# One fused layer on one core: lane chain ahead of the last four tiles, half of the gated sums on TensorE, 21 load buffers, 60 scatters over a stage border

## The chip, the cores and the metric

The kernel runs on one NeuronCore of a Trainium2 chip. The metric is the device time of one execution in microseconds (us); the median of three runs of the kernel before is 5569.49 us (5564.7 to 5574.14). The engines are called PE (TensorE matmul; PEld its weight loads), DVE (VectorE), ACT (ScalarE), POOL (GpSimd) and SP (SyncE, which here only issues transfers). A q behind an engine's name (SPq, ACTq) is its queue of transfers.

## The reference, cut to what matters

There are 12,500 nodes of 256 features and 212,500 edges sorted by destination. What concerns the change is the last part: every node is sent through four experts, and a graph attention over the edges (4 heads, 4 values a head) gives the scores by which the best two experts are weighted.

```python
xn = _layernorm(x); x = x + gnn(xn, edges) + mix(xn[None])[0]
x_flat = _layernorm(x)
h = (x_flat @ W_gat).reshape(M, HEADS, NUM_EXPERTS)
a_src, a_dst = (h * att_src).sum(-1), (h * att_dst).sum(-1)
e = leaky_relu(a_src[src] + a_dst[dst], 0.2)
ee = exp(e - segment_max(e, dst)[dst])
agg = segment_sum(h[src] * ee, dst) / segment_sum(ee, dst) + b_gat
w = softmax(top_k(_layernorm(agg).mean(heads), 2))
out = sum(g[e] * (gelu(x_flat @ W1[e] + b1[e]) @ W2[e] + b2[e]) for e in experts)
x = x + out
```

## The kernel before, in words

The nodes are 100 tiles of 125 rows (`NT`, `NP`). The program is a row of blocks with a barrier of all engines between them: a short setup, a graph stage (about 200 to 2801 us) in which POOL fetches the rows of the edges' sources (L773) while PE, DVE and ACT sum them, do the mixing layer and sort the edges, and a last block (from 2811 us).

In the graph stage each finished tile leaves 28 numbers a node for the router (`router_row`, L918 to L921). At its end POOL issues one scatter a tile (`ad_rows`, L778), which writes the destination's part of the score to every edge's place; the scatters t = 0 to 99 stand behind the last row fetch, each waits for its own tile.

In the last block four chains run side by side, each engine in the order of its own code:
- PE does 25 groups of four tiles: the first expert layer in 16 chunks (L1660, two matmuls each), then the second layer, 16 matmuls a tile (L1668). ACT's gelu (L1629) turns a chunk into `hid`; DVE adds the bias (L1603) and SP stores the tile's four expert outputs, 512 KB, to `y_rows` (L1295).
- POOL fetches the routers' rows of all sources (`nb`, L1339): 1024 gathers in 16 batches of 64, over `NBUF` = 3 buffers. `AHEAD` = 4 semaphores bound how many are in flight. A buffer comes free when DVE's `records` of its batch has read it (L1414).
- DVE does `scores(b)` at the tile `unit_after(b)` and `records(b)` one tile later: a running maximum, ACT's Exp, 20 scans over the lane (L1418). The records go to HBM. The tiles are 8, 16, 20, 25, 32, 36, 44, 48, 53, 60, 65, 72, 76, 84, 88 and 93.
- After batch 15 the lane chain joins the 128 lanes (functions `lane_ends`, `over_lanes`, `lane_sums`, `first_maxima`, `first_records`), one piece a tile at tiles 94 to 98, with four PE transposes (L1674) ahead of the last group's first layer, two (L1679, L1680) after its first tile, and two small Exp on ACT. It ends in a fetch and a scatter of one record a lane on POOL (L1345, L1348).

Then comes the tail. POOL fetches each tile's last records (`res`, L1355), SP loads the nodes' own rows (`own`, L1309). `weigh(k)` on DVE makes the gates of 20 tiles (`FT`), with three ACT functions between. `combine(t)` on DVE is four scalar-times-tensor-plus-tensor instructions (L1589) over the tile's four expert outputs (L1312) and residual (L1313), which SP loads into `YR` = 8 buffers once all y stores have landed. ACT's queue stores the result (L1649, two transfers a tile) from `AR` = 4 buffers.

## Time and profile before

| what | value |
|---|---|
| median of three runs | 5569.49 us |
| profiled execution, time and span | 5532.89 us, 5531.1 us |
| granted clock over the span | 0.804 |
| PE busy | 3498.8 us, 63% |
| POOL busy | 2828.8 us, 51% |
| DVE busy | 2089.8 us, 38% |
| ACT busy | 793.1 us, 14% |
| HBM read and written | 392.03 MB, 146.74 MB |

The busy shares are means over stages with different limits, so the rows below are taken by stage: the border of the two blocks, the groups of the last block with and without POOL's gathers, the last four tiles, and the tail in which PE no longer works. The times stand from the span's start.

### The profile page before, as it was taken

Reading aid. Unit: us, or ns where it says so; the run is one execution under the profiler, and the core shown is the slowest. Engines: PE = TensorE matmul, PEld = TensorE weight load, DVE = VectorE, ACT = ScalarE, POOL = GpSimd, SP = SyncE. Lnnn points to the kernel's source line nnn. Section 1 sums busy time; section 2 is a strip of 40 time slices with the busy share of each in tenths; the row PEclk is TensorE's granted clock in tenths of the full one; section 3 lists DMA queues with packets and bytes.
Section 4 is the critical chain, followed back from the end, with each engine's and each line's share of the span. In section 5 each row is a group of like instructions: output and inputs, shape, how many; then the busy total and the mean of one; then the engine's idle time right before and its main releaser. Section 6 shows DMA issues by size and latency. Waiting matters only on the chain.

```text
span 5531.1 us, 46201 instructions
## 1 busy us (share of the span) xinstructions
PE 3498.8 (63%) x12938; PEld 2286.8 (41%) x12938; DVE 2089.8 (38%) x4906; ACT 793.1 (14%) x1914; POOL 2828.8 (51%) x2951
## 2 busy tenths in 40 slices
PE   0688888888577777777242766666666666669300
PEld 0455555555455545555121443434343434346200
DVE  5466665566466545444110111202021111103288
ACT  4111111111011111111010101111111111112000
POOL 2666666666666666666657044445445353530420
PEclk6799999899788889888575888787778878789755
DMA  7444444444355555555121011111111111111287
GB/s 241 127 116 114 114 114 114 111 115 113 109 137 147 149 143 157 167 150 147 23 57 19 32 49 33 47 35 44 38 43 46 36 46 36 46 31 63 85 258 258
DMA packets 381412, 540.56 MB, mean 98 GB/s; under 512 B 120314, under 2 KB 297818, under 8 KB 381143
## 3 DMA queue, kind: packets, MB, share of 16 engines
q0 software_dynamic: 119136, 234.44, 17.7%
q1 hardware_dynamic: 239503, 284.45, 15.8%
q10 hardware_dynamic: 22632, 20.15, 1.1%
q8 instruction: 45, 0.74, 0.1%
q14 instruction: 96, 0.79, 0.0%
HBM read 392.03 MB, written 146.74 MB: 97 GB/s over the span
## 4 chain that ended last, share of the span: by engine, by line
PE 24%; another core or an unknown queue 13%; issue 7%; DVE 3%; DVEq 2%; DMA 1%; ACT 0%; SPq 0%; ACTq 0%
PE PS L1668 14%; PE PS L1660 10%; DVE acc L1589 2%; DVEq L1588 1%; DMA out<-acc 1%; ACT hid L1629 0%; DMA x2g<-x_turned 0%; DVE rec L1418 0%; DVE y_sb L1603 0%; DVE sc L1553 0%; SPq L1287 0%; DVE rden L1528 0%; ACTq L1649 0%; DVE q L1523 0%
## 5 line engine op out<-in xcount | busy, mean ns | idle before, releaser
L773 POOL DMA_INDIRECT rows<-xn_rows,gsrc x1664 | 1606.2, 965 | 881.2 <-issue 455.9
L1339 POOL DMA_INDIRECT nb<-route_rows,idx x1024 | 999.6, 976 | 1082.8 <-DVE msg L1414 767.7
L1668 PE MATMUL PS<-arena,hid 128*125 128x256 f32 x3200 | 771.0, 400 | 555.6 <-ACT hid L1629 339.4
L1078 PE MATMUL PS<-rows,oh 128*128 128x257 f32 x3328 | 891.2, 421 | 281.5 <-issue 207.2
L1660 PE MATMUL PS<-x2g,arena 128*128 128x500 f32 x1600 | 754.6, 631 | 284.8 <-issue 148.3
L1668 PEld LDWEIGHTS PS<-arena,hid 128*125 128x125 f32 x3200 | 632.8, 199 | 710.7 <-issue 578.9
L1603 DVE TENSOR_TENSOR y_sb<-PS,b_b 125x512 f32<-125x512 f32 x200 | 128.7, 685 | 2004.6 <-PE PS L1668 1467.7
L1078 PEld LDWEIGHTS PS<-rows,oh 128*128 128x128 f32 x3328 | 684.9, 212 | 411.3 <-issue 242.9
L1660 PEld LDWEIGHTS PS<-x2g,arena 128*128 128x128 f32 x1600 | 319.6, 203 | 698.7 <-issue 535.7
L1629 ACT ACTIVATE hid<-PS,b_sb 128x500 f32<-128x500 f32 x400 | 270.3, 677 | 1547.5 <-PE PS L1660 758.5
L1150 PE MATMUL PS<-own_w,p_t 128*125 128x512 f32 x400 | 237.2, 678 | 124.4 <-issue 68.8
L814 DVE TENSOR_TENSOR oh<-PS,rel 128x1024 f32<-128x1024 f32 x208 | 254.0, 1221 | 9.8 <-issue 1.8
L1095 PE MATMUL PS<-arena,x_t 128*125 128x512 f32 x400 | 223.3, 686 | 1.9 <-issue 1.9
L827 DVE TENSOR_REDUCE ss<-sq 125x16 f32<-125x1024 f32 x100 | 121.7, 1217 | 271.9 <-ACT sq L1028 193.6
L1097 PE MATMUL PS<-arena,x_t 128*125 128x512 f32 x400 | 191.0, 600 | 0.6 <-issue 0.6
L844 DVE TENSOR_TENSOR oh_lo<-PS,arena 128x500 bf16<-128x500 f32 x256 | 171.3, 669 | 0.0
L844 DVE TENSOR_TENSOR oh_hi<-PS,arena 128x400 bf16<-128x400 f32 x256 | 144.5, 564 | 61.0 <-remote 44.9
L1589 DVE SCALAR_TENSOR_TENSOR acc<-arena,gate,acc 125x256 f32<-125x256 f32 x300 | 145.4, 485 | 35.6 <-issue 14.0
L1022 ACT ACTIVATE kept<-PS 128x257 f32<-128x257 f32 x104 | 40.2, 386 | 827.8 <-remote 708.4
L1355 POOL DMA_INDIRECT res<-rec_rows,end_i x100 | 96.7, 967 | 116.0 <-DVE q L1523 84.9
L1113 PE MATMUL PS<-oh_lo,oh_hi 128*100 128x125 bf16 x1024 | 103.0, 235 | 76.1 <-issue 45.7
L1027 ACT ACTIVATE sq<-PS 125x512 f32<-125x512 f32 x100 | 59.7, 597 | 607.6 <-PE PS L1097 345.3
(303 smaller groups left out, 3093.0 us busy)
## 6 DMA issues: line engine op xcount, KB each, us to landing
y_rows<-y_sb SPq DMA_DIRECT2D x100, 512.0 KB
arena<-y_rows SPq DMA_DIRECT2D x100, 512.0 KB
rows<-xn_rows,gsrc POOLq DMA_INDIRECT x1664
nb<-route_rows,idx POOLq DMA_INDIRECT x1024
sum_rows<-kept SPq DMA_DIRECT2D x104, 128.5 KB
x_rows<-x SPq DMA_DIRECT2D x100, 128.0 KB
hid<-x_rows SPq DMA_DIRECT2D x100, 128.0 KB
m_in<-sum_rows SPq DMA_DIRECT2D x100, 125.5 KB
```

The lines of the kernel that those rows point to most:

```text
L773: pool.indirect_dma_start(out=rows[w][h][:, q, 0:D], out_offset=None, in_=xn_rows, in_offset=bass.IndirectOffsetOnAxis(ap=gsrc[:, s * HU + ...
L814: v.tensor_tensor(oh[w][h][:], NUMBERS.rearrange("p (o n) -> p o n", o=1).broadcast_to([P, HU, P]), along(rel[h][:], P), ALU.is_equal).the ...
L844: last = v.tensor_tensor(to[:, 4 * h:4 * h + 4, :], NUMBERS[:, 0:n].rearrange("p (o n) -> p o n", o=1).broadcast_to([P, 4, n]), along(of[: ...
L1078: last = mm(SUM[:, 0:D + 1], oh[w][h][:, q, :], rows[w][h][:, q, :], start=h == 0 and q == 0, stop=h == 1 and q == HU - 1)
L1095: mm(KP[0:NP, :], x_t[u][:, k * NP:(k + 1) * NP], wkv[:, k, 0:INNER], start=k == 0, stop=k == 1)
L1097: last = mm(VP[u][0:NP, :], x_t[u][:, k * NP:(k + 1) * NP], wkv[:, k, INNER:2 * INNER], start=k == 0, stop=k == 1)
L1150: both = lambda k: mm(GM[u][0:NP, :], p_t[q][:, k * NP:(k + 1) * NP], own_w[:, k, :], start=k == 0, stop=k == 1)
L1339: pool.indirect_dma_start(out=nb[b % NBUF][:, c, :], out_offset=None, in_=route_rows, in_offset=bass.IndirectOffsetOnAxis(ap=idx[:, b * W ...
L1589: last = v.scalar_tensor_tensor(out=acc[t % AR][:], in0=y_in[q][0:NP, e * D:(e + 1) * D], scalar=gate[:, t, e:e + 1], in1=acc[t % AR][:] i ...
L1629: a(hid[:, c, :], HP[c % 4][:, 0:4 * NP], ACT.Gelu, bias=b1_sb[:, c:c + 1]).then_inc(s_hid, 1)
L1660: last = mm(HP[c % 4][:, 0:4 * NP], w1_sb[:, k, e, (c % 4) * P:(c % 4 + 1) * P], x2g[u][:, k, :, :].rearrange("p j n -> p (j n)"), start=k ...
L1668: last = mm(Y[j % 2][e // 2][0:NP, (e % 2) * D:(e % 2 + 1) * D], hid[:, 4 * e + k, j * NP:(j + 1) * NP], w2_sb[:, e, k, :], start=k == 0, ...
```

## The change

It has six parts.
- **Scatters.** `ADS_EARLY` = 40: the scatters of tiles 0 to 39 stay in the graph stage, those of 40 to 99 stand at the start of the last block on POOL, ahead of the first `nb` gather. SP's load of what they wrote moves from the head of its queue to the sixth tile's store, and DVE's `start_ad` from tile 5 to tile 9 (by `unit_after(0)` - 3).
- **Batches.** `unit_after` now gives the tiles 12, 17, 24, 29, 36, 41, 48, 53, 60, 68, 72, 80, 84, 92 and 93, and sets the last batch behind all tiles; it is done with the lane chain. `AHEAD` is 8. `records` drains DVE between its 20 scans.
- **Lane chain.** `LANES_AT` = 96: behind tile 95's copy DVE does the last batch's scores and records and the whole chain in one piece; ACT does the batch's Exp ahead of the last group's gelus; PE's transposes (`turn_ends`) stand between the last group's two layers. `weigh(0)` stands ahead of the copies of tiles 98 and 99.
- **Gated sum.** In the tail, for every even tile ACT writes four diagonal matrices (the identity times a gate), PE multiplies them with the tile's four outputs into a PSUM bank, and DVE adds the residual in one instruction. Odd tiles are as before. `FT` is 10, and `weigh(k + 1)` stands ahead of the tiles of group k.
- **Buffers.** `YR` is 21 (five of their own, the others in space that is free by then), `AR` is 10, waited for by threes and pairs; the first five y tiles and `own(0)` are loaded at tile 95.
- **Queues.** `own(k + 2)` is loaded by ACT's queue and no longer by SP's. The stores of a tile stand ten tiles later on it.

Besides, `sort_low` and `sort_high` of the graph stage stand at other places of DVE's half step.

```diff
-YR = 8
-AR = 4
-FT = 20
+SPARE = 5
+YR = SPARE + 16
+AR = 10
+FT = 10
-AHEAD = 4
+AHEAD = 8
+ADS_EARLY = 40
+LANES_AT = NT - 4
 def unit_after(b):
-    t = int((b + 1) * 5.65) + 3
-    return t if t % 4 < 2 else t + 4 - t % 4
+    t = int((b + 1) * 6.06 + 5.5)
+    t = t if t % 4 < 2 else t + 4 - t % 4
+    return NT if b == NB - 1 else min(t, LANES_AT - 3)
...
-                for t in range(NT):
+                for t in range(ADS_EARLY):
                     pool.wait_ge(s_hc, t + 2)
...
+                    if t == 6:
+                        sp.wait_ge(s_ads, 16 * NT)
+                        sp.dma_start(ad[:], ad_rows[0:EF, :].rearrange("(p f) h -> p f h", p=P)).then_inc(s_adl, 16)
...
+                    if t == LANES_AT - 1:
+                        for b in late:
+                            store_records(sp, b)
+                        load_own(sp, 0)
+                        for i in range(AT_PE):
+                            load_y(i)
...
+                for t in range(ADS_EARLY, NT):
+                    pool.indirect_dma_start(out=ad_rows, out_offset=bass.IndirectOffsetOnAxis(ap=start_i[:, t:t + 1], axis=0),
+                                            in_=ad_all[:, t, :], in_offset=None).then_inc(s_ads, 16)
...
                     for k in range(20):
+                        if k:
+                            v.drain()
...
+                def add_rows(t):
                     q = t % YR
+                    dve.wait_ge(loaded(t), in_group(t))
                     if t >= AR:
+                        dve.wait_ge(stored(t), (t // AR) * 64)
+                    if t % 2 == 0:
+                        dve.wait_ge(s_cmb, t // 2 + 1)
+                        v.tensor_tensor(acc[t % AR], CMB[t // 2 % CB][0:NP, 0:D], x1_in[q][0:NP, :], ALU.add).then_inc(s_acc, 1)
+                        return
...
+                    if t == LANES_AT - 1:
+                        for b in late:
+                            scores(b)
+                            records(b)
+                        lane_ends()
+                        over_lanes()
+                        lane_sums()
+                        first_maxima()
+                        first_records()
+                    if t == NT - 3:
+                        weigh(0)
                 for k in range(FG):
-                    weigh(k)
+                    if k + 1 < FG:
+                        weigh(k + 1)
                     for t in range(k * FT, (k + 1) * FT):
-                        combine(t)
+                        add_rows(t)
...
+                        if t == k * FT:
+                            act.wait_ge(s_gt, k + 1)
+                            if k + 2 < FG:
+                                load_own(act, k + 2)
+                        if t % 2 == 0:
+                            if t // 2 >= DG:
+                                act.wait_ge(s_cmb, t // 2 - DG + 1)
+                            for e in range(NE):
+                                last = a(diag[t // 2 % DG][:, e, :], ident[0:NP, 0:NP], ACT.Copy, scale=gate[:, t, e:e + 1])
+                            last.then_inc(s_diag, 1)
+                        if t >= FT:
+                            store_out(t - FT)
...
+                def turn_ends():
+                    pe.wait_ge(s_ends, 1)
+                    for k in range(4):
+                        last = nc.tensor.transpose(HP[0][0:20, k * P:(k + 1) * P], ends[:, k, :], ident)
+                    last.then_inc(s_endt, 1)
+                    pe.wait_ge(s_ends, 2)
+                    nc.tensor.transpose(HP[1][:, 0:20], fm[:, 0:P], ident[0:20, 0:20])
+                    nc.tensor.transpose(HP[1][:, 20:40], fx[:, 0:P], ident[0:20, 0:20]).then_inc(s_endt, 1)
...
+                    if isinstance(g, int) and 4 * g == LANES_AT:
+                        turn_ends()
...
+                for t in range(0, NT, 2):
+                    pe.wait_ge(loaded(t), in_group(t))
+                    pe.wait_ge(s_diag, t // 2 + 1)
+                    if t // 2 >= CB:
+                        pe.wait_ge(s_acc, t - 2 * CB + 1)
+                    for e in range(NE):
+                        last = mm(CMB[t // 2 % CB][0:NP, 0:D], diag[t // 2 % DG][:, e, :], y_in[t % YR][0:NP, e * D:(e + 1) * D], start=e == 0, stop=e == NE - 1)
+                    last.then_inc(s_cmb, 1)
```

How the instructions stand on an engine is shown by its list in program order: line, operation, out<-in with the shape, semaphores waited for, and a count. First POOL at the border of the two blocks, before (L778 the scatters, L1339 the gathers of the first batch):

```order
L778 DMA ad_rows<-ad_all,start_i 143872x4 [waits s_hc] x100
L609 UNCONDITIONAL_BRANCH
L1325 UNCONDITIONAL_BRANCH [waits barrier_Pool_Activation_PE_DVE_SP_gather]
L1327 MEMSET first_e 125x16
L1329 AFFINE_SELECT first_e<-first_e 125x16 [waits s_fe]
L1331 DMA ad_first<-route_rows,first_i 128x28
L1339 DMA nb<-route_rows,idx 128x28 x4
```

And POOL at the same border after the change (L787 and L1369 the scatters, L1379 the gathers):

```order
L787 DMA ad_rows<-ad_all,start_i 143872x4 [waits s_hc] x40
L618 UNCONDITIONAL_BRANCH
L1362 UNCONDITIONAL_BRANCH [waits barrier_Pool_Activation_PE_DVE_SP_gather]
L1364 MEMSET first_e 125x16
L1366 AFFINE_SELECT first_e<-first_e 125x16 [waits s_fe]
L1369 DMA ad_rows<-ad_all,start_i 143872x4 x60
L1371 DMA ad_first<-route_rows,first_i 128x28
L1379 DMA nb<-route_rows,idx 128x28 x8
```

Sixty scatters moved behind the barrier and ahead of the first gather.

PE in the last group before: the lane chain's transposes (L1674) stand ahead of the first layer (L1660; its first chunk waits for DVE's copy of them, s_endc), and L1679 and L1680 behind the first tile of the second layer (L1668).

```order
L1668 MATMUL PS<-arena,hid 125x256 x15
L1674 MATMUL PS<-wide,ends 20x128 [waits s_ends]
L1674 MATMUL PS<-wide,ends 20x128 x3
L1660 MATMUL PS<-x2g,arena 128x500 [waits s_hid,s_x2l0,s_endc]
...
L1668 MATMUL PS<-arena,hid 125x256 x15
L1679 MATMUL PS<-wide,fm 128x20 [waits s_fx]
L1680 MATMUL PS<-wide,fx 128x20
L1668 MATMUL PS<-arena,hid 125x256 [waits s_yc]
```

PE in the last group after, from the end of the first layer (L1745) over the second (L1755) to the first gated sums (L1773):

```order
L1745 MATMUL PS<-x2g,arena 128x500
L1733 MATMUL PS<-wide,ends 20x128 [waits s_ends,s_hid]
L1733 MATMUL PS<-wide,ends 20x128 x3
L1736 MATMUL PS<-wide,fm 128x20 [waits s_ends]
L1737 MATMUL PS<-wide,fx 128x20
L1755 MATMUL PS<-arena,hid 125x256 [waits s_yc]
...
L1773 MATMUL PS<-spare_y,nb 125x256 [waits s_diag,s_yl0,s_yc]
L1773 MATMUL PS<-spare_y,nb 125x256 x3
```

All six transposes now stand between the two layers, and the second layer's 64 matmuls are behind both waits for DVE (s_ends).

DVE after, from the copy of tile 97 (L1649) to the first tiles of the tail: weigh(0) begins at L1548 and ends with the gates at L1620, L1630 is an even tile, L1635 an odd one.

```order
L1649 TENSOR_TENSOR y_sb<-PS,b_b 125x512
L1548 TENSOR_TENSOR zf<-res,own 125x40 [waits s_res0,s_own]
...
L1620 TENSOR_TENSOR gate<-sx,m 125x40
L1649 TENSOR_TENSOR y_sb<-PS,b_b 125x512 [waits s_ys0,s_y]
...
L1620 TENSOR_TENSOR gate<-sx,m 125x40
L1630 TENSOR_TENSOR nb<-PS,hid 125x256 [waits s_cmb,s_yl0]
L1635 SCALAR_TENSOR_TENSOR nb<-spare_y,gate,hid 125x256 [waits s_yl0]
L1635 SCALAR_TENSOR_TENSOR nb<-spare_y,gate,nb 125x256 x3
```

Before, all of `weigh` stood behind the copy of tile 99; now the copies of tiles 98 and 99 are behind the wait for the first `own` and `res`.

## Rows read from the trace of the kernel before

**Rows 1.** Costliest groups of the page: operation, count | busy, mean ns | idle, releaser
```profile
L1339 POOL DMA_INDIRECT nb<-route_rows,idx x1024 | 999.6, 976 | 1082.8 <-DVE msg L1414 767.7
```

**Rows 2.** Windows: start:end, us, busy PE, PEld, DVE, ACT, POOL, PEclk, DMA, GB/s
```profile
2822.00:2852.00 30.00, 29.07 (x63) 13.05 (x64) 0.00 (x0) 9.41 (x13) 20.74 (x22) 0.89 0.29 89
2852.00:3064.00 212.00, 46.55 (x99) 25.43 (x97) 2.58 (x4) 2.71 (x4) 156.58 (x165) 0.53 0.11 19
3091.00:3192.00 101.00, 99.38 (x339) 63.48 (x338) 24.54 (x37) 23.58 (x34) 0.00 (x0) 1.00 0.13 45
...
5250.00:5531.00 281.00, 0.00 (x0) 0.00 (x0) 234.00 (x537) 13.93 (x20) 39.23 (x40) 0.50 0.81 258
5173.00:5531.00 358.00, 0.00 (x0) 0.00 (x0) 255.03 (x590) 17.41 (x25) 91.64 (x95) 0.50 0.72 226
```

**Rows 3.** Timeline inside the first burst: start, us, engine, line, [idle before <-releaser]
```profile
2899.20 0.59 PE L1668 MATMUL PS<-arena,hid 128*125 128x256 f32 x1 [2.42 <-issue]
...
2902.00 0.59 PE L1668 MATMUL PS<-arena,hid 128*125 128x256 f32 x1 [2.21 <-issue]
```

**Rows 4.** What POOL's gathers (L1339) waited for: us, times
```profile
  DMA nb<-route_rows,idx: 13.8, 23
```

**Rows 5.** The scatters of the border (L778): ns min/median/max, first and last start
```profile
L778 POOL DMA_INDIRECT ad_rows<-ad_all,start_i x100: 965/969/1053, 2620.8 to 2800.9; - x100
...
  issue: 27.4, 90
```

**Rows 6.** Timeline of the last eight tiles, columns as in rows 3
```profile
5074.95 27.89 PE L1668 MATMUL PS<-arena,hid 128*125 128x256 f32 x128 [0.77 <-ACT hid L1629]
...
5090.27 0.16 DVE L1385 COPY m_run<-m_run 128x4 f32<-128x4 f32 x1
...
5096.14 0.63 ACT L1633 ACTIVATE dd<-dd 128x512 f32<-128x512 f32 x1 [19.94 <-DVE dd L1401]
...
5099.64 5.32 DVE L1418 TENSOR_TENSOR_SCAN rec<-dd,rec,msg 128x64 f32<-128x64 f32 x20
...
5105.52 1.03 PE L1674 MATMUL PS<-wide,ends 128*20 128x128 f32 x4 [2.67 <-DVE ends L1432]
...
5108.35 29.04 PE L1660 MATMUL PS<-x2g,arena 128*128 128x500 f32 x64 [1.81 <-DVE endt L1448]
...
5111.40 0.42 ACT L1636 ACTIVATE dc<-dc 20x256 f32<-20x256 f32 x1 [14.63 <-DVE dc L1463]
```

**Rows 7.** Timeline from the last tile into the tail
```profile
5166.44 0.97 POOL L1355 DMA_INDIRECT res<-rec_rows,end_i  x1 [1.51 <-DMA rec_rows<-fix,put_i]
...
5168.84 1.29 DVE L1603 TENSOR_TENSOR y_sb<-PS,b_b 125x512 f32<-125x512 f32 x2 [5.19 <-issue]
...
5173.20 4.57 SPq L1312 DMA_DIRECT2D arena<-y_rows  x1
```

**Rows 8.** Timeline of the tail's steady part, columns as in rows 3
```profile
5252.31 0.48 DVE L1589 SCALAR_TENSOR_TENSOR acc<-arena,gate,hid 125x256 f32<-125x256 f32 x1
...
5254.39 0.48 DVE L1589 SCALAR_TENSOR_TENSOR acc<-arena,gate,hid 125x256 f32<-125x256 f32 x1
...
5269.01 7.67 SPq L1312 DMA_DIRECT2D arena<-y_rows  x1
...
5283.41 0.23 DVE L1506 TENSOR_TENSOR zf<-res,own 125x80 f32<-125x80 f32 x1
```

**Rows 9.** Timeline, first tile after the second weigh
```profile
5300.45 0.48 DVE L1589 SCALAR_TENSOR_TENSOR acc<-arena,gate,hid 125x256 f32<-125x256 f32 x1 [0.15 <-issue]
```

**Rows 10.** Groups by line: operation, count | busy, mean ns | idle before
```profile
L900 DVE TENSOR_TENSOR x<-x,PS 125x256 f32<-125x256 f32 x100 | 42.2, 422 | 7.5
...
L1016 ACT ACTIVATE x_t<-PS 128x250 f32<-128x250 f32 x100 | 39.8, 398 | 53.4 <-PE PS L1087 37.0 <-remote 16.5
...
L1044 ACT ACTIVATE ssq<-ssq 125x1 f32<-125x1 f32 x100 | 20.3, 203 | 6.8
```

**Rows 11.** Out stores on ACT's queue (L1649): ns min/median/max
```profile
L1649 ACTq DMA_DIRECT2D out<-acc x200: 322/371/1539, 5233.6 to 5529.1; - x100
```

More of the change, by code:

```diff
@@ L1325, in _ @@
+                for q in range(AR // 2):
+                    sp.wait_ge(s_out[q], 64 * NT // AR)
             @block.gpsimd
@@ L1497, in first_records @@
                     v.drain()
[L1498 removed]
+                    v.tensor_tensor(fix[:, 0:20], fix[:, 0:20], back[:, 1, :], ALU.add).then_inc(s_fix, 1)
                 def weigh(k):
```

154 lines of the change are left out of this document (80 added, 74 removed).

## The prediction

> **What bounds the kernel now.** I read the page's groups first, then windows cut at the borders of the stages, then the timelines of the last tiles and of the tail; a mean over the whole span would mix four different limits. In the last block PE is the bound where POOL is quiet: it is busy 99.38 of 101 us in the window from 3091 [rows 2]. Where POOL runs a long row of gathers, PE is not the bound and not waited for either: after the first 30 us of such a row (29.07 busy) it does 46.55 us of work in 212 [rows 2], and the reader is to see its matmuls 2.80 us apart with "issue" as the only reason [rows 3]. So a long row of POOL transfers costs PE about 0.78 of what lies behind its first 30 us. From 5173 on PE has nothing, the granted clock is 0.50 (the 1.2 GHz level), and two limits run close together: DVE is busy 234.0 of 281 us, the transfers 0.81 at 258 GB/s [rows 2]. A tile takes DVE 2.07 us (5252.31 to 5254.39), one `weigh` of 20 tiles 17.04 us (5283.41 to 5300.45) [rows 8, 9].
>
> **The zero of the sum.** Tile 95's matmuls end at 5074.95 + 27.89 = 5102.84 [rows 6]. Seen from there the span before ends at 5531.1 - 5102.84 = +428.3, and the y loads begin at 5173.20, +70.4 [rows 7].
>
> **The border of the stages.** Ninety scatters stand back to back, each 0.969 us and an issue gap of 27.4 / 90 = 0.30, so 1.27 us apart [rows 5]; the last ten come with their tiles. With 40 scatters, 50 of the ninety leave, 64 us. The engines' part behind them (2734 to 2801) shifts forward by about that, since PE, DVE and ACT stood nearly still meanwhile. In the last block 60 x 1.27 = 76 us stand ahead of the gathers. POOL's first row so ends 12 us later; but PE now starts on the first group 64 us earlier and works at 46.55 / 212 = 0.22 during the 76 us more, 17 us of work. The sum is 12 - 17 = -5, and I take 0 with 10 to each side. `ad` and `start_ad` come later, by tile 6 and tile 9; they have until tile 12.
>
> **Batches, eight in flight, drains.** POOL waited for its own gathers 23 times, 13.8 us of 1082.8 idle [rows 1, 4]; nearly all the rest is DVE's `records`. Eight in flight can win at most these 13.8. The thirteen later rows of 64 stay thirteen, at other tiles: 0, with 10 to each side for the cover that each finds. The drains make the 20 scans longer: 5.32 us is 0.27 a scan now, overlapped [rows 6]; apart, a step of DVE of this size takes near 0.46 (an addition of 0.42 and its gap), so 19 x 0.19 = 3.6 us a batch, hidden on DVE, which does little between two copies of PE's tiles; only the last batch shows it. Moving the sorts in DVE's half step of the graph stage changes the order, not the work: 0, with 10 to each side.
>
> **The lane chain.** Before: last tile's copy at 5168.84, first `res` at 5166.44 [rows 7]. After, from tile 95: `records(14)` ends about +6, the copy +7.3, `scores(15)` takes 5.9 (5090.27 to 5096.14 [rows 6]) to +13.2, Exp 0.63 and a table load until +15.4. Until then no gelu of the last group runs, and PE has only four PSUM banks for its first layer; it stalls 8.6 us behind chunk 4. (The layer before took 29.04 with about 2 us of such a stall.) The first layer so ends about +36.2, `hid` +36.9. `records(15)`, 8.7 with drains 12.3, is done by then. The transposes, the pieces between and the small Exp took from 5105.52 to 5111.82 [rows 6], 6.3 us, and the sums another 0.6: PE waits 6.9 us, to +43.8, and ends its four tiles 27.9 later at +71.7, against +66.0. What waits behind: only these four tiles. The record's fetch and scatter go ahead beside them; the first `res` starts about +50, ten have landed at +65. `weigh(0)` takes to +81, then come the copies of tiles 98 and 99 (+84) and the loads at +86.3: 16 us later than before. Price of a `weigh` of ten tiles: between half of 17.04 and all of it; its instructions are many and short, so I take 12.8.
>
> **The tail.** `own(1)` lands about +93, and `weigh(1)`, with ACT's first matrices ahead of its Exp, ends at +114. From there on DVE has 50 odd tiles at 2.07, and 50 even ones: one addition of 125x256 from PSUM, 0.42 [rows 10], 0.50 with its gap. That is 50 x 2.57 = 128.5; eight more `weigh` 102.4; 2.4 for the last store: +347. Ten us for waits (nothing to 26, which is 0.1 of the window) give +357.
> ACT's side: a diagonal matrix is 125x125, between the 0.203 us of a one-column and the 0.398 of a 250-column instruction [rows 10], I take 0.30; four of them and four stores at 0.371 [rows 11] are 2.7 us a pair, with both bounds 2.3 to 3.1. This is as long as DVE's pair of 2.57; but ACT goes on during `weigh`, so it sets nothing unless it is at the upper end, 50 x 0.5 = 26 us. PE's side: 27.89 / 16 = 1.74 us for four matmuls at full clock, 3.5 at the clock 0.50 of the tail: 17.5 a group against DVE's 25.6.
> Transfers: 0.72 x 358 = 258 us of full work before [rows 2], less about 8 for the five y tiles loaded ahead, 250. Between +86 and +347 they would have to be busy 0.96; with +357, 0.92. With 8 buffers they reached 0.81, in a window where SP's queue stood 7.67 us on the y load behind `own` [rows 8]; 21 buffers and `own` on another queue are there to bridge this. I take 0.92.
>
> On that queue a rule of the Trainium skill bears (DMA: Bandwidth & Descriptors, "Issuing engines are not separate DMA queues"): whichever engine starts a transfer, it runs on the same 16 engines, and another issuer saves only issue time. By it the move of `own` is worth nothing; were the hold of 7.67 us wholly gone each time, it would be ten such holds, and the sum above counts none of them.
>
> **The sum.** -71 us in the last part (+428.3 to +357), 0 elsewhere. The profiled execution took 5532.9, so 5462; the median of the runs shown stands 36.6 above it, and I forecast 5569.5 - 71 = 5498.
>
> **Rivals.**
> A. The transfers stay where they were, 0.81: 250 / 0.81 = 309 from +86, +395. It gains 33: 5536. For it: the share did not follow DVE's load, and more loads and stores in flight share the same engines. Against: before, a load could go out only when one of 8 buffers came free, and there were stretches in which none was.
> B. Slower: eight gathers in flight take PE's cover. If the first 30 us of each row shrink because POOL's gathers are issued closer, or because more of them are under way, PE loses 0.78 x 15 = 12 us a row at half the cover, 13 rows 152 us: -71 + 152 = +81, 5650. It decides above 5.5 us a row. Against: POOL issues one each 1.25 us and waited for a landing only 23 times [rows 4].
> C. ACT, PE and DVE run one after another: ACT's Exp of the next `weigh` stands behind the group's matrices and stores, which wait for PE's sums and DVE's tiles. With 8 us lost in each of nine groups, 72 us, nothing is gained: 5570. For it: ACT's pair is as long as DVE's. Against: PE's 17.5 us a group have 25.6.
> D. POOL's rows do not slow PE by what they issue. The scatters moved over the border would cost the last block nothing while the graph stage is 64 us shorter: 5498 - 64 = 5434. Against: PE's 46.55 us in 212 stand right beside them [rows 2].
> The Trainium skill (Runtime: NRT & Kernel Launch, "Instruction fetch mechanics") says that instructions are fetched ahead by a queue of each engine's own and that this is hidden; by it D would hold. The trace does not agree: 2.80 us between matmuls of 0.59 [rows 3].
>
> **Chances.** Forecast 0.52, A 0.22, D 0.08, C 0.08, B 0.08, and 0.02 for a border that costs more than the tail gives. A measurement of this kernel tells 0.2% (11 us) from nothing: faster 0.82, the same 0.08, slower 0.10. The forecast's own range is 5470 to 5525, by the waits (0 to 26), ACT's upper end and the border; with A and D and their own spread 5430 to 5560, which leaves out C's upper half and B.
>
> **What would show it.** Right: PE's last second layer begins 44 us behind tile 95 and the loads 86; the last block opens about 64 us earlier and its first group ends where it did, within 10; DVE's tail has pairs of about 2.6 us with no wait of more than 1 us ahead of an even tile, and a transfer share above 0.9. Wrong in the tail: "DMA" or PE's sum (L1773) as the releaser of most tiles. Wrong in the groups: rows of 64 in which PE slows before its twentieth us. The prediction fails as a whole if the border is not neutral, since there 60 to 76 us stand against each other.

## The result and the profile after

The changed kernel takes 5612.55 us (median of 4 runs, 5608.44 to 5618.63) against 5569.4 (5564.7 to 5574.14) before: 1.0078 times, interval 1.0065 to 1.009. It is 43 us slower; 71 us faster was forecast, and the time lies above the range.

The table holds this and every later run. The stages are cut at the same instructions in each kernel: *rows* from the first to the last row fetch of the graph stage, *border* from there to the first group's last copy, *groups* to tile 91's copy, *last 8* to tile 99's copy, *tail* to the end (us). The last column is of the 13 later rows of 64 gathers: from a row's start to the end of the last gelu that comes in time, which is the last one before a gap of over 2 us (median), and how many gelus (chunks of the first layer) ACT does in all 13. All are worked out from the traces. The ratio is to the kernel before, run in the same set (several kernels and that one, on one chip). That kernel took 5569.4, 5526.19, 5560.91, 5533.57, 5560.59 and 5535.58 us in the six sets, so kernels of different sets are compared by ratio.

| kernel | ratio (interval) | rows | border | groups | last 8 | tail | late gelu / gelus |
|---|---|---|---|---|---|---|---|
| before | 1 | 2485 | 473 | 1955 | 121 | 362 | 22.4 / 176 |
| after | 1.0078 (1.0065-1.009) | 2513 | 480 | 2031 | 153 | 304 | 17.3 / 113 |
| after_again | 1.0085 (1.0068-1.0102) | 2508 | 476 | 2029 | 153 | 304 | 17.3 / 116 |
| e1_no_drains | 0.9976 (0.996-0.9991) | 2478 | 474 | 1959 | 145 | 304 | 20.7 / 174 |
| e2_ahead4 | 1.0040 (1.0024-1.0055) | 2498 | 480 | 1983 | 153 | 310 | 15.7 / 136 |
| e3_old_sorts | 1.0041 (1.0023-1.0058) | 2469 | 476 | 1998 | 153 | 316 | 15.7 / 129 |
| e4_before_drains | 1.0074 (1.0054-1.0094) | 2481 | 468 | 1982 | 126 | 363 | 15.5 / 128 |
| e5_own_sp | 1.0031 (1.0016-1.0046) | 2514 | 478 | 2028 | 153 | 276 | 17.2 / 116 |
| e6_ads100 | 1.0098 (1.0077-1.0119) | 2508 | 475 | 2024 | 153 | 300 | 15.8 / 116 |
| e7_all_dve | 1.0169 (1.0148-1.0189) | 2501 | 478 | 2033 | 153 | 357 | 17.2 / 113 |
| c1_four_undone | 0.9882 (0.9865-0.99) | 2470 | 479 | 1948 | 145 | 277 | 22.4 / 179 |
| c2_ahead8 | 0.9900 (0.9884-0.9917) | 2474 | 482 | 1959 | 145 | 272 | 20.7 / 175 |
| c3_weigh_behind | 0.9883 (0.9864-0.9902) | 2473 | 485 | 1954 | 144 | 277 | 22.5 / 181 |
| c4_new_sorts | 0.9906 (0.9891-0.9921) | 2486 | 479 | 1950 | 145 | 277 | 22.4 / 180 |
| d1_drains_ahead | 0.9900 (0.9883-0.9917) | 2514 | 480 | 1965 | 148 | 272 | 23.9 / 180 |
| d2_longer_dve | 0.9727 (0.971-0.9743) | 2507 | 480 | 1859 | 154 | 271 | 27.4 / 203 |
| d3_with_drains | 1.0017 (1.0007-1.0027) | 2509 | 479 | 2022 | 153 | 274 | 16.5 / 119 |
| d4_with_drains_ahead8 | 1.0020 (1.001-1.0031) | 2504 | 479 | 2029 | 152 | 271 | 16.5 / 117 |
| f1_pause16 | 0.9428 (0.9401-0.9454) | 2484 | 476 | 1696 | 153 | 275 | 22.4 / 209 |
| f2_pause8 | 0.8622 (0.8607-0.8638) | 2484 | 329 | 1237 | 304 | 278 | no late gelu |

The forecast's 71 us were a gain of 89 in the tail (273 us, from the copies at +84 to the end at +357, against 362) less 18 in the last eight tiles (+84 against +66). The tail won 58, the last eight tiles lost 32, and the groups lost 76 where nothing was expected. These are differences of two profiled executions: the one of before took 5532.9 us, 36.6 under its median, the one after 5618.6, and the stages together differ by 86 us where the medians differ by 43. So the groups' 76 can be more than the change costs there, and prices are taken from the ratios. (The rows stage stands 44 us apart in c1 and d1, which do the same in it on two chips, and 20 in e1 and e2 on one; single differences there are not read.)

The gathers of the last block (columns as in [rows 1]) and windows (as in [rows 2]) of the changed kernel: POOL's first row, a stretch in which POOL is quiet, the tail.

```profile
L1379 POOL DMA_INDIRECT nb<-route_rows,idx x1024 | 985.2, 962 | 1280.5 <-DVE msg L1454 972.2
```
```profile
2799.00:3096.00 297.00, 68.78 (x127) 33.03 (x125) 2.58 (x4) 6.10 (x9) 227.22 (x230) 0.54 0.12 15
3128.00:3285.00 157.00, 154.53 (x532) 99.84 (x532) 30.31 (x47) 34.47 (x50) 0.00 (x0) 1.00 0.17 60
5313.00:5617.00 304.00, 125.73 (x400) 91.91 (x400) 196.78 (x594) 93.74 (x245) 74.76 (x77) 0.69 0.82 259
```

In the first row PE does 68.78 us of work in 297, 0.23 of it, as the 0.22 of [rows 2]; with POOL quiet it is busy 154.53 of 157. Those two readings held. DVE is busy 196.78 of the tail's 304, less than the 234.0 of 281 of [rows 2]; the transfers reach 0.82, not 0.92.

What the groups lost shows in one later row of 64, which begins at 3592.75 before and at 3581.41 after. ACT's gelus in it (start, us, engine, line, [idle before <-releaser]), before and after:

```profile
3610.94 0.68 ACT L1629 ACTIVATE hid<-PS,b_sb 128x500 f32<-128x500 f32 x1 [1.00 <-PE PS L1660]
3612.62 0.68 ACT L1629 ACTIVATE hid<-PS,b_sb 128x500 f32<-128x500 f32 x1 [1.00 <-issue]
3615.84 0.68 ACT L1629 ACTIVATE hid<-PS,b_sb 128x500 f32<-128x500 f32 x1 [2.55 <-remote]
3627.08 0.68 ACT L1629 ACTIVATE hid<-PS,b_sb 128x500 f32<-128x500 f32 x1 [7.03 <-remote]
3638.27 0.68 ACT L1629 ACTIVATE hid<-PS,b_sb 128x500 f32<-128x500 f32 x1 [10.51 <-remote]
...
3660.67 0.68 ACT L1629 ACTIVATE hid<-PS,b_sb 128x500 f32<-128x500 f32 x1 [10.52 <-remote]
```
```profile
3594.48 1.28 ACT L1694 ACT_TABLE_LOAD   x1 [16.45 <-remote]
3598.02 0.68 ACT L1694 ACTIVATE hid<-PS,b_sb 128x500 f32<-128x500 f32 x1 [2.26 <-remote]
3602.97 0.68 ACT L1694 ACTIVATE hid<-PS,b_sb 128x500 f32<-128x500 f32 x1 [4.27 <-remote]
3610.00 0.68 ACT L1694 ACTIVATE hid<-PS,b_sb 128x500 f32<-128x500 f32 x1 [6.35 <-remote]
3620.53 0.68 ACT L1694 ACTIVATE hid<-PS,b_sb 128x500 f32<-128x500 f32 x1 [9.85 <-remote]
```

Before, they come 1.68 us apart until 3612.62, 20 us into the row, and only then farther and farther apart. After, the first one is 16.6 us into the row and already late. (The two rows begin at different points of a group: PE's first layer starts 2.9 us into the row before and, by its own rows, 9.8 after. Most rows of before start as the latter, and in those the first late gelu comes 23 us or more into the row.) "remote" names no releaser in this program. PE's rows in the same row before:

```profile
3595.65 26.99 PE L1660 MATMUL PS<-x2g,arena 128*128 128x500 f32 x64
3661.48 9.57 PE L1668 MATMUL PS<-arena,hid 128*125 128x256 f32 x35 [38.84 <-ACT hid L1629]
```

All 64 records of the first layer's 16 chunks lie before 3622.64: PE runs up to four chunks ahead of ACT, one for each PSUM bank. The last four gelus read sums that are ready and still come 11.2 us apart, and PE's 38.84 us are a wait for the last of them, at 3660.67. So the late engine here is ACT, and the gelus are counted.

DVE at the end of that batch's `records`, after and in the kernel without drains:

```profile
3581.23 8.97 DVE L1460 TENSOR_TENSOR_SCAN rec<-dd,rec,msg 128x64 f32<-128x64 f32 x20
3590.10 1.28 DVE L1649 TENSOR_TENSOR y_sb<-PS,b_b 125x512 f32<-125x512 f32 x2
```
```profile
3522.55 5.32 DVE L1458 TENSOR_TENSOR_SCAN rec<-dd,rec,msg 128x64 f32<-128x64 f32 x20
3527.76 1.28 DVE L1647 TENSOR_TENSOR y_sb<-PS,b_b 125x512 f32<-125x512 f32 x2
```

The scans take 8.97 us for 5.32 (as in [rows 6]): +3.65, the 3.6 of the prediction. POOL at the start of the row, before (with DVE's scans there) and after:

```profile
3592.58 5.32 DVE L1418 TENSOR_TENSOR_SCAN rec<-dd,rec,msg 128x64 f32<-128x64 f32 x20
3592.75 0.99 POOL L1339 DMA_INDIRECT nb<-route_rows,idx  x1 [37.20 <-DVE msg L1414]
3594.05 1.00 POOL L1339 DMA_INDIRECT nb<-route_rows,idx  x1 [0.30 <-issue]
3595.36 3.33 POOL L1339 DMA_INDIRECT nb<-route_rows,idx  x1 [0.30 <-issue]
3598.99 0.94 POOL L1339 DMA_INDIRECT nb<-route_rows,idx  x1 [0.30 <-issue]
```
```profile
3581.41 1.00 POOL L1379 DMA_INDIRECT nb<-route_rows,idx  x1 [86.66 <-DVE msg L1454]
3582.71 1.05 POOL L1379 DMA_INDIRECT nb<-route_rows,idx  x1 [0.30 <-issue]
3584.07 1.05 POOL L1379 DMA_INDIRECT nb<-route_rows,idx  x1 [0.30 <-issue]
3585.42 1.05 POOL L1379 DMA_INDIRECT nb<-route_rows,idx  x1 [0.30 <-issue]
```

Before, the third gather is held for 3.33 us and ends at 3598.69, 0.8 us after the 20 back-to-back scans; with a drain between the scans none is held. It is a pause in POOL's issuing, six microseconds into the row, that the drains took away.

### The profile page after: what moved, and what is told of

The parts are those of the page before. It is cut to its first block, busy times and chain, and to the rows that moved or that the text cites. A ratio compares the mean times of both kernels' runs of the same rounds, so it can differ in the third digit from the quotient of the medians.

```text
span 5616.7 us, 47651 instructions
## 1 busy us (share of the span) xinstructions
PE 3708.8 (66%) x13337; PEld 2411.3 (43%) x13338; DVE 2074.5 (37%) x4946; ACT 860.6 (15%) x2135; POOL 2819.1 (50%) x2951
## 4 chain that ended last, share of the span: by engine, by line
PE 20%; another core or an unknown queue 13%; issue 11%; DVE 3%; ACT 1%; DVEq 1%; DMA 1%; SPq 1%; ACTq 0%
PE PS L1755 11%; PE PS L1745 9%; DVE nb L1635 1%; ACT hid L1694 1%; DVEq L1634 0%; ACTq L1682 0%; SPq L1322 0%; ACT nb L1719 0%; DVE rec L1460 0%; DMA ad<-y_rows 0%; ACT L1694 0%; DMA arena<-y_rows 0%; DVE z L1404 0%; DVE m_run L1428 0%
## 5 line engine op out<-in xcount | busy, mean ns | idle before, releaser
L1379 POOL DMA_INDIRECT nb<-route_rows,idx x1024 | 985.2, 962 | 1280.5 <-DVE msg L1454 972.2
L1745 PE MATMUL PS<-x2g,arena 128*128 128x500 f32 x1600 | 844.2, 685 | 604.1 <-ACT hid L1694 306.2
L1086 PE MATMUL PS<-rows,oh 128*128 128x257 f32 x3328 | 921.2, 433 | 285.9 <-ACT kept L1030 147.0
L1755 PE MATMUL PS<-arena,hid 128*125 128x256 f32 x3200 | 747.2, 392 | 348.3 <-issue 181.2
L1649 DVE TENSOR_TENSOR y_sb<-PS,b_b 125x512 f32<-125x512 f32 x200 | 128.7, 686 | 2099.1 <-PE PS L1755 1681.6
L1086 PEld LDWEIGHTS PS<-rows,oh 128*128 128x128 f32 x3328 | 708.0, 219 | 425.3 <-issue 213.4
L1755 PEld LDWEIGHTS PS<-arena,hid 128*125 128x125 f32 x3200 | 619.1, 194 | 488.7 <-issue 349.6
L1745 PEld LDWEIGHTS PS<-x2g,arena 128*128 128x128 f32 x1600 | 337.2, 218 | 1093.8 <-issue 693.5
L1113 PE MATMUL PS<-k_sb,v_sb 125*128 125x128 f32 x800 | 119.9, 298 | 73.0 <-DVE v_sb L845 54.2
```

What stands on the lines that cost most here:

```text
L1086: last = mm(SUM[:, 0:D + 1], oh[w][h][:, q, :], rows[w][h][:, q, :], start=h == 0 and q == 0, stop=h == 1 and q == HU - 1)
L1379: pool.indirect_dma_start(out=nb[b % NBUF][:, c, :], out_offset=None, in_=route_rows, in_offset=bass.IndirectOffsetOnAxis(ap=idx[:, b * W ...
L1649: last = v.tensor_tensor(y_sb[t % 2][0:NP, half * 512:half * 512 + 512], Y[t % 2][half][0:NP, :], b2_b[:, half * 512:half * 512 + 512], AL ...
L1745: last = mm(HP[c % 4][:, 0:4 * NP], w1_sb[:, k, e, (c % 4) * P:(c % 4 + 1) * P], x2g[u][:, k, :, :].rearrange("p j n -> p (j n)"), start=k ...
L1755: last = mm(Y[j % 2][e // 2][0:NP, (e % 2) * D:(e % 2 + 1) * D], hid[:, 4 * e + k, j * NP:(j + 1) * NP], w2_sb[:, e, k, :], start=k == 0, ...
```

## Experiments

The first four share a set. The changed kernel was not run in it, so a difference to the changed kernel is one of two ratios on two chips (1.0078 in the first set, 1.0085 in the one of after_again). The theories are named in words where they are judged. Where an expectation speaks of PE's cover, that is the time from a row's start to PE's first gap over 2 us in the trace: 30.3 us before, 20.6 after, 30.8 in c1, 34.3 in d2, 64.3 in f1 (means of 13 rows). The gelus of the table are the more direct measure, since PE runs ahead of ACT and then waits for it.

**e1_no_drains**, of the changed kernel:
```diff
-                        if k:
-                            v.drain()
```


> The changed kernel without the drains between the 20 scans of records; all else as changed. Theory 1 (the drains keep DVE 12.2 us a batch in place of 8.5, and PE, which has two pairs of PSUM banks for its tiles, waits for the copies): the scans take about 5.3 us again, the tiles behind a batch no longer take 12 to 13 us, PE's stall behind chunk 4 of the last group shrinks from 19 to about 9 us, and the time falls by some 60 to 85 us, to about 5530 to 5550. Theory 2 (eight gathers in flight shorten PE's cover in a row of 64): the rows cost what they do now, about 61 us each, and the time falls by less than 25 us.

Measured 0.9976, 0.0102 or 56 us below the changed kernel. The groups take 1959 us again, with 174 gelus in the rows for 113: the drains are the largest loss. In the set itself e3, with drains and with the old order of the sorts, stands 0.0065 or 36 us above e1. DVE's lateness alone could be that price, 13 x 3.65 = 47 us; d1 and d2 part the two. In the last group drains cost by lateness alone. PE at tile 95 and behind it, after and without drains:

```profile
5215.41 6.87 PE L1745 MATMUL PS<-x2g,arena 128*128 128x500 f32 x16
5241.62 21.86 PE L1745 MATMUL PS<-x2g,arena 128*128 128x500 f32 x48 [19.34 <-ACT hid L1694]
```
```profile
5101.38 6.87 PE L1743 MATMUL PS<-x2g,arena 128*128 128x500 f32 x16
5120.14 21.91 PE L1743 MATMUL PS<-x2g,arena 128*128 128x500 f32 x48 [11.89 <-ACT hid L1692]
```

The stall behind chunk 4 is 19.34 us with drains and 11.89 without: two batches of scans stand there, 2 x 3.65 = 7.3.

**e2_ahead4**, of the changed kernel:
```diff
-AHEAD = 8
+AHEAD = 4
```


> The changed kernel with four gathers in flight in place of eight. Theory 1 (drains): within 10 us of the changed kernel, 5612. Theory 2 (eight in flight): about 5 us less for each of 13 rows, 5545 to 5560.

Measured 1.0040: 21 us better by the ratios. But e3, which keeps eight in flight and has the old sorts, comes out the same on this chip, and its groups take 1998 us against 1983 here; so the 21 us may be the chip's. In c2 eight in flight cost 7 us and in d4 nothing.

**e3_old_sorts**, of the changed kernel, the two sorts back at the end of DVE's half step:
```diff
-                    (0, 0, SORTED_AT, sort_low),
...
-                    (2, 0, NT, spread), (0, 0, SORTED_AT, sort_high),
+                    (2, 0, NT, spread),
...
+                    (0, 0, SORTED_AT, sort_low), (0, 0, SORTED_AT, sort_high), (0, 0, SORTED_AT, sort_turn)], plain=SORTED_AT)
```


> The changed kernel with the two sort steps at their old places in DVE's half step of the graph stage. The profile of the changed kernel reaches the last row gather of the graph stage 29 us later than that of before. Theory 3 (the new order of the sorts delays each half step): 20 to 29 us faster, and the last row gather starts near 2620. Rival (the profile of before was a short one, 37 us under its median, and the order is neutral): within 10 us of 5612, last row gather between 2620 and 2650.

Measured 1.0041, 20 us better than the changed kernel; but the groups, in which nothing is sorted, are 33 us shorter, so this run alone does not show it: an unlike edit, e2, gives the same on the same chip. c4 asks again.

**e4_before_drains**, of the kernel before:
```diff
                     for k in range(20):
+                        if k:
+                            v.drain()
```


> The kernel before with the drains between the 20 scans of records added, nothing else. Theory 1: it gets slower by 40 to 80 us (5610 to 5650), with the same 12 to 13 us at the tiles behind a batch. Theory 2 or 3: within 15 us of 5569. Its graph stage is that of before, so its profile also shows how far that stage's length moves from run to run.

Measured 1.0074, +34 us; the gelus in the rows fall from 176 to 128, the first late one comes at 15.5 us for 22.4. The drains cost this with none of the change beside them.

The next four share a set; **after_again** is the changed kernel with no edit (5606.34 us).

> The changed kernel once more, for runs on the same chip as the three others and a second profile. All theories: 1.0065 to 1.009 times the kernel before. Its profile tells how far the graph stage's length (last row gather at 2648.5 us in the first profile) moves from run to run.

Measured 1.0085, and the groups and the tail within 3 us of the first trace.

**e5_own_sp**, of the changed kernel, `own` by SP's queue among the y loads:
```diff
+                    if t == 2 * FT:
+                        load_own(sp, 2)
...
+                    if t % FT == 0:
+                        load_own(sp, t // FT)
...
-                            if k + 2 < FG:
-                                load_own(act, k + 2)
```


> The changed kernel with the own rows of groups 2 to 9 loaded by SP's queue again (at tiles 20, 30, ... of its loads), no longer by ACT's. In the changed kernel the store behind such a load holds ACT up to 20 us, and DVE then waits for ACT's Exp in the next weigh, 53 us in all nine. Theory 4 (the hold moved from SP's queue, where it only delayed loads, onto the engine that DVE waits for): DVE's waits for that Exp fall below 20 us and the time by 20 to 45 us against the changed kernel. Rival (the transfers set the tail, and any wait of DVE is only where they show): within 10 us of it.

Measured 5581.01 against after_again's 5606.34: 25 us better, the tail 276 for 304. ACT and its queue in the changed kernel, behind an `own`:

```profile
5351.53 0.29 ACTq L1303 DMA_DIRECT2D own<-route_rows  x1
5351.98 20.36 ACTq L1682 DMA_DIRECT2D out<-nb  x1
5373.95 0.40 ACT L1719 ACTIVATE nb<-wide,gate 125x125 f32<-125x125 f32 x1 [20.81 <-issue]
```

The store right behind `own` holds ACT's issuing 20.36 us, and the next diagonal matrix stands behind the stores (20.81 us of idle, "issue"). DVE's `weigh` waits for ACT's Exp, after and here (waits in the tail: engine, line, releaser: us, times, longest):

```profile
DVE q L1562 <- ACT df L1705: 53.1, 9, 24.0
```
```profile
DVE q L1566 <- ACT df L1709: 7.5, 9, 3.6
```

One row of SP's queue here, and the tail's window:

```profile
5336.02 14.02 SPq L1322 DMA_DIRECT2D hid<-x_rows  x1
```
```profile
5307.00:5584.00 277.00, 124.80 (x401) 90.24 (x400) 197.07 (x594) 89.86 (x234) 74.64 (x78) 0.74 0.91 284
```

The hold is still there, 14.02 us on the load behind `own`, but the tail no longer shows it: DVE's waits for ACT are short and the share is 0.91.

**e6_ads100**, of the changed kernel, all scatters back in the graph stage:
```diff
-ADS_EARLY = 40
+ADS_EARLY = 100
```


> The changed kernel with all 100 scatters in the graph stage again. Theory 5 (the border is neutral, the 64 us that leave one side are paid on the other): within 12 us of the changed kernel; from the last row gather to the end of the first group 465 to 485 us as in both kernels. Rival (moving them costs, since the first group waits for POOL's longer row): 15 us or more faster; rival D of the prediction: 50 us or more slower.

5606.94 against 5606.34: nothing, and the border 475 for 476. The border is neutral, and rival D, by which this kernel would be 50 us or more slower, is out.

**e7_all_dve**, of the changed kernel, even tiles as odd ones, ACT's diagonal matrices and PE's sums left out:
```diff
-                    if t % 2 == 0:
-                        dve.wait_ge(s_cmb, t // 2 + 1)
-                        v.tensor_tensor(acc[t % AR], CMB[t // 2 % CB][0:NP, 0:D], x1_in[q][0:NP, :], ALU.add).then_inc(s_acc, 1)
-                        return
```


> The changed kernel with the even tiles' gated sum on DVE too, as for the odd ones; ACT's diagonal matrices and PE's sums are gone. Theory 6 (DVE's own work, with its waits for ACT, sets the tail): 50 x 1.57 = 78 us more work on DVE, less the waits for ACT's Exp that vanish with the matrices (up to 50): 25 to 60 us slower than the changed kernel. Rival (the transfers set the tail): within 15 us of it.

5658.27: +52. The tail's window, which answers to the changed kernel's:

```profile
5299.00:5657.00 358.00, 0.54 (x3) 0.13 (x1) 272.53 (x744) 30.37 (x45) 82.04 (x78) 0.51 0.69 221
```

DVE is busy 272.53 of 358: it does 76 us more work, the tail is 53 us longer, and the transfers' share falls to 0.69. So DVE sets the tail without TensorE's sums, and 21 buffers without them win nothing (357 for 362 before, with `own` on ACT's queue).

**c1_four_undone** undoes e1, e2, e3 and e5's parts at once, of the changed kernel:
```diff
-AHEAD = 8
+AHEAD = 4
...
-                            v.drain()
...
+                        load_own(sp, t // FT)
...
+                    (0, 0, SORTED_AT, sort_low), (0, 0, SORTED_AT, sort_high), (0, 0, SORTED_AT, sort_turn)], plain=SORTED_AT)
```


> The changed kernel with four of its parts undone together: no drains between the scans, four gathers in flight, the sort steps at their old places, own rows by SP's queue. Left are the lane chain ahead of the last tiles, the scatters over the border, half of the gated sums on TensorE, groups of ten, 21 buffers. If the four costs measured one by one (54, 16, 20 and 25 us) add up, it is 115 us under the changed kernel and 60 to 80 us under the kernel before (ratio 0.986 to 0.989). Rival (they share one cause, so that undoing one takes most of the others): 30 us under the kernel before, or less.

Measured 0.9882: 65 us faster than before. What is left of the change does about what was forecast for it. PE in the last group and the tail's window:

```profile
5086.88 6.87 PE L1745 MATMUL PS<-x2g,arena 128*128 128x500 f32 x16
5105.64 23.21 PE L1745 MATMUL PS<-x2g,arena 128*128 128x500 f32 x48 [11.89 <-ACT hid L1696]
```
```profile
5176.00:5454.00 278.00, 122.73 (x402) 88.88 (x400) 196.60 (x594) 90.80 (x237) 75.24 (x78) 0.73 0.91 284
```
```profile
DVE zf L1550 <- DMA own<-route_rows: 34.6, 4, 10.8
```

The span is 5453.3, so the end is 366.4 behind tile 95 (+428.3 before, +357 predicted, 401.3 in the changed kernel), with the transfers' share at 0.91. DVE's waits for `own`, 34.6 us in four, are its longest in the tail.

The next three, in c1's set, put back or move one thing of c1. **c2_ahead8** and **c4_new_sorts**:
```diff
-AHEAD = 4
+AHEAD = 8
```


> As the kernel with four parts undone, but with eight gathers in flight. If eight in flight cost by themselves: 10 to 20 us slower than it. If they cost only together with the drains (the stage of the groups took 1959 us without drains at eight in flight, as before at four): within 6 us of it.

0.9900 against 0.9882, 7 us. The intervals overlap, but all five runs (5468.8 to 5481.16) lie above all of c1's (5455.47 to 5466.24).

```diff
+                    (0, 0, SORTED_AT, sort_low),
...
+                    (2, 0, NT, spread), (0, 0, SORTED_AT, sort_high),
```


> As the kernel with four parts undone, but with the sort steps at the changed kernel's places. If their order costs by itself: 12 to 25 us slower than it, all of it between the first and the last row gather of the graph stage. If what the single run showed was the chip's spread: within 6 us.

0.9906, 13 us worse than c1; the intervals overlap a little, the runs do not (5473.57 to 5478.35 against 5455.47 to 5466.24). e3 has the same sign, with 20. Two waits of the graph stage in c1 and in c4 (columns as in e5):

```profile
DVE ss L836 <- ACT sq L1036: 127.0, 45, 9.7
POOL rows L782 <- PE PS L1088: 114.7, 28, 7.4
```
```profile
DVE ss L836 <- ACT sq L1036: 183.3, 50, 10.4
POOL rows L782 <- PE PS L1088: 130.6, 30, 7.6
```

DVE waits 56 us more for ACT's squares and POOL's fetches 16 us more for PE. That a sort of 0.69 us ahead of the one-hot matrix reaches the fetches by way of PE is read from these waits; no run shows it by itself.

**c3_weigh_behind**, `weigh(0)` behind the last copies:
```diff
-                    if t == NT - 3:
-                        weigh(0)
+                weigh(0)
```


> As the kernel with four parts undone, but with the first weigh behind the copies of tiles 98 and 99. The last two y stores and so the loads of the tail begin some 13 us earlier, and the second weigh no longer waits 10 us for its own rows: 5 to 13 us faster than it. Rival (the first weigh is then the later one and sets the start of the tail): 0 to 8 us slower.

0.9883, nothing. The last copies wait for PE: tile 98's comes 14.2 us behind tile 97's, for 7.0 us of matmuls, which stand up to 2.1 us apart there while POOL fetches the first `res`.

The next four, of c1 again, part the drains' three effects: more instructions, a later DVE, POOL no longer held. **d1_drains_ahead** puts 19 drains where they hold up nothing between the scans, ahead of the release of POOL's row:
```diff
+                    for _ in range(19):
+                        v.drain()
```


> The kernel with four parts undone, with 19 drains in records ahead of the instruction that frees POOL's buffer, and none between the scans: as many more instructions on DVE as the changed kernel has, but all before the row of 64 gathers begins. Theory 7 (instructions that DVE has to take during a row of gathers shorten PE's cover in it, the time from the row's start until PE's first gap over 2 us): the cover stays near 30 us and the time within 8 us of the kernel with four parts undone (0.988 of the kernel before). Theory 1 (DVE late with its copies, wherever the time goes): some us a batch, as far as 19 drains in a row take time. If drains anywhere cost: 30 to 55 us slower.

0.9900, +10 us by the ratios; 180 gelus, POOL's third gather held as before. Drains as such are not the cause. Whether 19 more instructions inside the row, as the drains between the scans are, cost anything besides the lost hold, this run does not tell.

**d2_longer_dve** makes DVE late without parting the scans, by four writes of 128x1024 ahead of them:
```diff
+                    if b < NB - 1:
+                        for q in range(4):
+                            v.memset(spare_y[q][:], 0.0)
```


> The kernel with four parts undone, with four memsets of 128x1024 (0.91 us each, 3.6 us in all, on a space that nobody reads then) ahead of the scans of each batch but the last: DVE is as late as with the drains, by 4 instructions in place of 19. Theory 7 (the number of instructions): cover 27 to 30 us, time within 12 us of the kernel with four parts undone. Theory 1 (the time DVE takes): cover 20 to 25 us and 25 to 45 us slower.

0.9727, 85 us faster than c1 though DVE is 4.1 us later a batch. The theory that DVE's later copies are the price falls with it. POOL at one of its rows:

```profile
3556.74 1.05 POOL L1383 DMA_INDIRECT nb<-route_rows,idx  x1 [0.30 <-issue]
3558.10 3.34 POOL L1383 DMA_INDIRECT nb<-route_rows,idx  x1 [0.30 <-issue]
3561.74 0.95 POOL L1383 DMA_INDIRECT nb<-route_rows,idx  x1 [0.30 <-issue]
```

The hold moved from the third gather to the sixth and ends 10.1 us into the row (5.9 in c1), both as medians of the 13 rows; the last gelu in time ends at 27.4 (22.4 in c1). That is 17.3 and 16.5 us from the end of the hold (14.8 to 18.0 in the other kernels with one); in the kernels without a hold it is 15.5 to 17.3 from the row's start. The ranges agree, which leaves little for the 19 instructions themselves. So the theory left is that the engines' cover counts from POOL's last pause. There are 203 gelus in the rows for 179. Counted by PE's records of both layers (27.0 us a group for the first, 27.9 for the second), PE loses 571 us in the 13 rows for 585 in c1, and 76 for 141 in the twelve stretches between them: 79 of the 85 us, most of it behind the rows.

**d3_with_drains** and **d4_with_drains_ahead8** put the drains back into c1, d4 with `AHEAD` = 8 as well:
```diff
+                        if k:
+                            v.drain()
```


> The kernel with four parts undone, with the drains between the scans put back (four gathers in flight). Theories 1 and 7 alike: cover 20 to 25 us, 30 to 55 us slower than the kernel with four parts undone, 0.994 to 0.998 of the kernel before.

> As the one with the drains put back, but with eight gathers in flight, on the same chip. If eight in flight cost together with the drains: cover 2 to 4 us shorter and 10 to 20 us slower than with four. If the 16 us found before were the chip's or chance: within 6 us.

1.0017 and 1.0020: the drains cost c1 0.0135, 75 us (65 against d1, which shares the set), and eight in flight nothing beside them. By the count used for d2, PE loses 669 us in d3's rows for 585 in c1, and 134 for 141 between them: 77 us.

**f1_pause16** and **f2_pause8** test the pause directly: in c1 POOL waits at every 16th, or every 8th, gather until all that it issued have landed. The gathers stay the same.
```diff
-                        if b or c >= AHEAD:
+                        if c % 16 == 0 and (b or c):
+                            for q in range(AHEAD):
+                                pool.wait_ge(s_nb[q], (b * W + c) // AHEAD * 16)
+                        elif b or c >= AHEAD:
```


> The kernel with four parts undone, but POOL waits at every 16th nb gather until all gathers in flight have landed, a pause of an estimated 1 to 2 us. Theory 8 (in a row of gathers PE's cover counts from the last pause in POOL's issuing: 24 us from the end of the 3.34 us hold of the third gather in the kernels without drains, 20 to 24 from the row's start in those with drains, which have no such hold; each pause lets the instructions catch up): a row of 64 with three pauses inside costs less than half of the 55 us that it costs now, the groups shrink by 300 us or more, and the time falls to 0.90 to 0.94 of the kernel before. Rival (a pause without a hold of POOL by DVE gives nothing, or is too short): 0 to 15 us slower than the kernel with four parts undone.

> The same with the wait at every 8th gather. Theory 8: at least the gain of every 16th, less some 20 us for longer rows if these set anything; if the pause is too short to give back the whole cover, more than every 16th gives. Rival: 0 to 30 us slower than the kernel with four parts undone.

0.9428 and 0.8622: f2 takes 4771.45 us, 764 less than before on its set, and is the best kernel of these. POOL in f2 and the window of 19 groups:

```profile
3309.64 0.95 POOL L1386 DMA_INDIRECT nb<-route_rows,idx  x1 [0.30 <-issue]
3312.80 0.95 POOL L1386 DMA_INDIRECT nb<-route_rows,idx  x1 [2.21 <-issue]
```
```profile
3003.00:4059.00 1056.00, 1039.84 (x3652) 686.23 (x3651) 256.51 (x614) 242.93 (x339) 671.23 (x672) 1.00 0.25 66
```

A pause of 2.21 us after each eight gathers (10 us), and PE is busy 1039.84 of 1056 us, 55.6 a group, at the granted clock 1.00 (the 2.4 GHz level) while POOL gathers 672 times. With 16 the pauses are as long but 20 us apart, beyond the 15 to 18 of the cover: in its 13 rows PE idles over 1.2 us between matmuls 95 times (in f2's once), 51 of them more than 15 us behind the last pause, and the gain on c1 is 0.045 for 0.126. The pauses cost POOL 302.7 us in 133 waits:

```profile
  POOL nb L1386: 302.7, 133
```
```profile
DVE m_run L1432 <- DMA nb<-route_rows,idx: 158.8, 2, 83.4
```

Now POOL is the late one: near the end DVE waits 158.8 us for its rows, which is the 304 of the last eight tiles.

## Why the prediction was wrong

- **The step that failed** is "3.6 us a batch, hidden on DVE, which does little between two copies of PE's tiles; only the last batch shows it". The 3.65 us were right and DVE did hide them. The price was elsewhere: parted scans no longer hold POOL's gather for 3.3 us, the late gelus begin 5 us sooner in 13 rows and a third of the gelus in them are gone, and the kernel pays 34 us in the kernel before (e4), 36 to 56 in the changed one (e1) and 65 to 75 in c1 (d3). Nor was it the last batch alone that showed it on DVE: two batches' scans stand in the last group's stall. The 3.33 us gather stood in the trace of before, in every one of these rows, and I had not asked what followed from it. The Trainium skill (SBUF — State Buffer, "SBUF: two separate sides") says that a transfer issued by GpSimd can't write its descriptors while VectorE runs an instruction that takes the port pair that the two share. The trace agrees with the hold, 3.33 us until the scans end; that this port is the reason no run here shows, and that the hold helps PE no page says.
- **Rival B** had the symptom, rows in which PE loses its cover, at 0.08; the drains' 34 to 75 us in 13 rows are 2.6 to 5.8 a row, beside its 5.5. Its cause, eight in flight, is at most a small part: 7 us in c2, nothing in d4, and the 21 of e2 may be the chip's.
- **"Changes the order, not the work: 0"** for the sorts is 13 us in c4, just past its own 10, and 20 in e3, not all of it theirs.
- **The hold behind `own`**: the queue was to "bridge this". On ACT's queue it stopped the matrices, Exp and stores instead, 25 us. This is rival C in part: ACT's Exp is late, by a transfer and not by its order of work. The Trainium skill's rule (DMA: Bandwidth & Descriptors, "Issuing engines are not separate DMA queues") would have the issuer save its own issue time alone, usually little; the trace differs, since ACT lost 20 us of issuing at one `own`. On SP the share is 0.91 (0.92 predicted) and the tail 276 (357 - 84 = 273).
- **The lane chain**: the stall was predicted at 8.6 and is 11.89 without drains, 19.34 with. `records(14)` was to end at +6; it ends at +9.6 without drains and +17.0 with. The second layer begins at +55 (5270.46 - 5215.41), +49 in c1, and not +44. Matmuls behind tile 97's copy stand up to 2.80 us apart beside POOL's `res`, `weigh(0)` takes 18.1 us there for 12.8, and the last copies come at +97, not +84.
- **Right**: the border (0 +- 10; e6 within 1 us), the tail's limit by DVE (e7, +52), and the sum of what c1 leaves: its end is 366.4 behind tile 95 where +357 stood, and its ratio 0.9882 is -65 us for -71. Two terms offset each other in part there: DVE's pair of tiles takes 2.41 us for 2.57, 8 us less in all, and its waits for `own` behind `weigh(1)` are 25 us where 10 stood for all waits. The parts that c1 undoes make up the rest of the miss: 75 for the drains, 25 for `own` and 13 for the sorts are 113 us, and c1 and the changed kernel are 0.0196 or 109 us apart.
- **Open**: what a pause of POOL's lets the other engines regain, and why it lasts 15 to 18 us on ACT. f1 and f2 wait until all gathers in flight have landed, so they do not part the pause from the empty queue; and no run gave the drained kernel its pause back without the scans. Why the drains cost 34 us in e4 and 65 in d3 was not asked. Whether a pause of another length or the row of 60 scatters with pauses gives more was not tried.

## What to carry to other kernels

Where one engine issues a long row of indirect transfers and others slow with "issue" or "remote" as the only reason, try short pauses in the row before moving work about: two microseconds in every twelve were worth nearly 13% of the time here (f2 against c1). A change that is "hidden" on an engine is to be followed to whom that engine held up before; a stall that vanishes may have been feeding someone. A transfer that holds its queue belongs on an engine that has nothing else to do.

## What the hardware showed that was not expected

- ACT's gelus come 1.68 us apart for 15 to 18 us behind the last pause of POOL's gathers, then 5 to 11 us apart, with PE's sums ready for them; with a pause of 2.2 us after each eight gathers (f2) none is late in the 13 rows.
- Twenty back-to-back scans on DVE hold one POOL gather for 3.3 us; with drains between them all gathers beside them take 1.05 us.
- A transfer on the queue behind `own` is held, 14.02 us on SP's and 20.36 on ACT's, and ACT's own instructions wait with it (20.81 us).
